# A causal mask moved from TensorE to VectorE, a subtraction from VectorE to GpSimd, and softmax exponents taken head by head with accumulated sums

## The reference

```
def _mha(x, kv, Wq, Wk, Wv, mask, causal):          # block 1: 16 heads of 8
    Q, K, V = (einsum('bsd,hdk->bhsk', t, W) * m ...)
    energy = einsum('bhsk,bhtk->bhst', Q, K)
    lengths = sum(energy[:, :, 0, :] != 0, axis=-1)
    energy = where(cols >= lengths, -inf, energy)
    if causal:
        energy = where(cols[None, :] > cols[:, None], -inf, energy)
    score = softmax(energy / sqrt(dk), axis=-1)
    return einsum('bhst,bhtk->bhsk', score, V) * m
x1 = layernorm(x + mha(x, x, Wq1, Wk1, Wv1, mask0, causal=True))
x2 = layernorm(x1 + mha(x1, context, Wq2, Wk2, Wv2, mask1, causal=False))
x3 = layernorm(x2 + ffn(x2))
# block 2: 16 heads of 64; bias and graph_attn_bias are the same input f
scores = einsum('bhqd,bhkd->bhqk', (x3 @ wq + bq) / 8, ctx @ wk + bk) + f + f
weights = softmax(scores, axis=-1)
out = layernorm(einsum('bhqk,bhkd->bhqd', weights, ctx @ wv + bv) @ wo + bo + x3)
```

## Time and profile before

| | |
|---|---|
| median of 3 runs | 341.50 us (341.49 to 341.51) |
| the profiled execution | 341.61 us, of which the trace spans 339.8 us |
| PE busy | 320.3 us, 94% of the span |
| DVE busy | 291.3 us, 86% |
| ACT busy | 239.9 us, 71% |
| POOL busy | 241.6 us, 71% |
| granted TensorE clock, mean | 0.995 |

### The profile page before, as it was taken

The page is one execution under the profiler, slowest core; times in us unless marked ns, Lnnn a source line. Parts: engine busy times, 40 slices in busy tenths (PEclk is TensorE's granted clock), DMA queues, the critical chain, the costliest instruction groups (busy, mean ns, idle before and its releaser), DMA issues.

```text
span 339.8 us, 13231 instructions
## 1 busy us (share of the span) xinstructions
PE 320.3 (94%) x5328; PEld 252.3 (74%) x5333; DVE 291.3 (86%) x836; ACT 239.9 (71%) x567; POOL 241.6 (71%) x376
## 2 busy tenths in 40 slices
PE   6799999999999989999999999999999999999982
PEld 2467668786869787878878787877878687867762
DVE  3776998999999999999999898989998989885661
ACT  1677768587787867778867876787785978776541
POOL 0453385676898858786978779687778679788773
PEclk9999999999999999999999999999999999999998
DMA  5996000010003000210100040001200040004001
GB/s 154 332 327 210 3 0 2 3 65 4 2 4 133 2 4 2 88 57 12 54 4 3 2 141 4 11 3 33 103 2 5 0 143 3 3 17 136 2 2 31
DMA packets 13180, 17.87 MB, mean 53 GB/s; under 512 B 1601, under 2 KB 10177, under 8 KB 13121
## 3 DMA queue, kind: packets, MB, share of 16 engines
q1 hardware_dynamic: 13120, 17.04, 15.8%
HBM read 15.99 MB, written 1.05 MB: 50 GB/s over the span
## 4 chain that ended last, share of the span: by engine, by line
PE 56%; DVE 26%; ACT 5%; issue 5%; POOL 4%; DMA 1%; SPq 1%; POOLq 0%; ACTq 0%; DVEq 0%
PE C_E L632 5%; PE C_E L577 4%; PE B_E L451 3%; PE C_E L622 3%; PE A_E L432 3%; PE B_E L432 3%; PE C_E L593 2%; DVE A_mx L889 2%; PE A_E L451 2%; DVE A_S L897 2%; PE C_E L609 2%; PE B_E L465 2%; DVE Sc L973 2%; DVE C_den L991 2%; DVE L_xh L943 2%
## 5 line engine op out<-in xcount | busy, mean ns | idle before, releaser
L1025 POOL TENSOR_TENSOR A_kblk<-A_qk,cst 128x1024 f32<-128x1024 f32 x16 | 30.3, 1897 | 25.5 <-DVE A_qk L865 25.4
L1046 POOL TENSOR_TENSOR L_xg<-L_xh,vec_sb 128x128 f32<-128x128 f32 x64 | 29.2, 456 | 15.9 <-DVE L_xh L943 13.9
L1035 POOL TENSOR_TENSOR L_rstd<-L_ve,cst 128x1 f32<-128x1 f32 x64 | 35.1, 548 | 5.0
L1077 POOL TENSOR_TENSOR Sc<-Sc,C_mx 128x512 f32<-128x512 f32 x28 | 29.1, 1046 | 9.4 <-DVE C_mx L983 9.3
L763 ACT ACTIVATE qT<-C_E,bq 128x128 f32<-128x128 f32 x112 | 31.9, 379 | 4.1 <-PE C_E L577 3.9
L1033 POOL TENSOR_TENSOR L_ve<-L_mv,cst 128x1 f32<-128x1 f32 x64 | 12.1, 189 | 29.4 <-DVE L_mv L930 28.8
L1086 POOL TENSOR_TENSOR Pc<-Pc,C_rd 128x512 f32<-128x512 f32 x28 | 29.0, 1043 | 2.8 <-DVE C_rd L993 2.5
L1025 POOL TENSOR_TENSOR B_kblk<-B_qk,cst 128x1024 f32<-128x1024 f32 x16 | 30.3, 1897 | 0.0
L577 PE MATMUL C_E<-x3T,wq_sb 128*128 128x128 f32 x224 | 29.6, 279 | 0.4 <-ACT x3T L755 0.4
L577 PEld LDWEIGHTS C_E<-x3T,wq_sb 128*128 128x128 f32 x224 | 27.0, 192 | 1.1 <-ACT x3T L755 0.7
L632 PE MATMUL C_E<-wo_sb,C_zT 128*128 128x128 f32 x224 | 27.5, 276 | 0.1
(11 more groups left out here) (186 smaller groups left out, 1002.4 us busy)
## 6 DMA issues: line engine op xcount, KB each, us to landing
f<-in_fs SPq DMA_DIRECT2D x16, 512.0 KB, 4.0
out<-osb SPq DMA_DIRECT2D x16, 64.0 KB, 1.8
cTs<-in_ctxT SPq DMA_DIRECT2D x1, 768.0 KB, 9.2
xTs<-in_xT SPq DMA_DIRECT2D x1, 768.0 KB, 6.8
xs<-in_x SPq DMA_DIRECT2D x1, 768.0 KB, 9.0
cs<-in_ctxn SPq DMA_DIRECT2D x1, 768.0 KB, 11.2
vec_sb<-in_vecs SPq DMA_DIRECT2D x1, 640.0 KB, 7.8
wk_sb<-in_wk SPq DMA_DIRECT2D x1, 512.0 KB, 4.5
```

The source lines that it names most:

```text
L1025: tt(a.kblk[:], a.qk[:, 1].unsqueeze(1).to_broadcast([P, 8, P]), at["rmask"].unsqueeze(2).to_broadcast([P, 8, P]), ALU.mult).then_inc(a.s_ ...
L1035: tt(l.rstd[:], l.ve[:], at["power"], ALU.pow).then_inc(l.s_rstd, 1)
L1046: tt(l.xg[:], l.xh[:], l.g, ALU.mult).then_inc(l.s_xg, 1)
L1077: tt(v, v, place(n).mx[:, 8 * g:8 * g + 8].unsqueeze(2).to_broadcast([P, 8, S]), ALU.subtract).then_inc(C.s_sub, 1)
```

## The change

Four edits, and a new `PLAN` for them:

- The mask is no longer added by PE. DVE adds `later` (now f32) to the scores as it moves them from PSUM to `A.S` (`A.msk_0`, `A.msk_1`), then takes the maxima from `A.S`, and the subtraction of the maxima, in place in `A.S`, goes to POOL (`a_sub`).
- In C's second half (`_1`), POOL no longer subtracts the maxima from 512 columns but multiplies the eight maxima by -2; ACT takes the exponents in eight ACTIVATEs of 64 columns with that as bias, and each also writes its head's sum (`accum_out`) to `den`; DVE then only takes the reciprocal. The first half (`_0`) stays as it was.
- `A.m0`'s comparison takes a tensor of zeros in place of the number 0.
- `COOL` goes from 6 to 9: nine `L.warm` steps of three products instead of six.

```diff
-COOL = 6
+COOL = 9
...
-            def energy(a, l, causal):
+            def energy(a, l):
...
-                                      a.kblk[r, :, S * b:S * b + S], start=True, stop=not causal,
-                                      skip_group_check=True)
-                    if causal:
-                        for hf, bank in enumerate((a.E, a.X)):
-                            r = slice(S * hf, S * hf + S)
-                            for b in range(2):
-                                last = mm(bank[S * b:S * b + S, :], eye64[r, :],
-                                          later[r, :].unsqueeze(1).to_broadcast([S, 8, S]),
-                                          start=False, stop=True, skip_group_check=True)
+                                      a.kblk[r, :, S * b:S * b + S], start=True, stop=True)
                     last.then_inc(a.s_e, 1)
...
             def c_exp(g):
                 def step(n):
+                    o = place(n)
+                    if g == 0:
+                        act.wait_ge(C.s_sub, 2 * n + 1)
+                        act.activation(o.P[:, 0:HALF], o.S[:, 0:HALF], ACT.Exp, scale=2.0).then_inc(C.s_p, 1)
+                    else:
+                        act.wait_ge(C.s_sub, 2 * n + 2)
+                        for h in range(8, 16):
+                            last = act.activation(o.P[:, h * S:(h + 1) * S], o.S[:, h * S:(h + 1) * S], ACT.Exp, scale=2.0,
+                                                  bias=o.mx[:, h:h + 1], accum_out=o.den[:, h:h + 1])
+                        last.then_inc(C.s_p, 1)
...
-                ts(m0s[:, n:n + FIRST], am0[:, n:n + FIRST], 0.0, None, ALU.is_gt).then_inc(s_m0, 1)
+                tt(m0s[:, n:n + FIRST], am0[:, n:n + FIRST], blank[:, 0:FIRST], ALU.is_gt).then_inc(s_m0, 1)
...
+            def masked(hf):
+                def step(n):
+                    dve.wait_ge(A.s_e, n + 1)
...
+                    tt(heads(A.S[:, hf * HALF:(hf + 1) * HALF]), heads((A.E, A.X)[hf][:, :]),
+                       later[:].unsqueeze(1).to_broadcast([P, 8, S]), ALU.add).then_inc(A.s_msk, 1)
+            def masked_max(hf):
+                def step(n):
+                    dve.wait_ge(A.s_msk, 2 * n + 1 + hf)
+                    dve.tensor_reduce(A.mx[:, 8 * hf:8 * hf + 8], heads(A.S[:, hf * HALF:(hf + 1) * HALF]), AX.X, ALU.max
+                                      ).then_inc(A.s_max, 1)
...
-                    dve.tensor_reduce(d, heads(place(n).P[:, g * HALF:(g + 1) * HALF]), AX.X, ALU.add).then_inc(C.s_den, 1)
-                    dve.wait_ge(C.s_den, 2 * n + 1 + g)
+                    if g == 0:
+                        dve.tensor_reduce(d, heads(place(n).P[:, 0:HALF]), AX.X, ALU.add).then_inc(C.s_den, 1)
+                        dve.wait_ge(C.s_den, n + 1)
                     dve.reciprocal(place(n).rd[:, 8 * g:8 * g + 8], d).then_inc(C.s_rd, 1)
...
                     pool.wait_ge(C.s_max, 2 * n + 1 + g)
+                    if g == 1:
+                        m = place(n).mx[:, 8:16]
+                        tt(m, m, at["twice"].to_broadcast([P, 8]), ALU.mult).then_inc(C.s_sub, 1)
+                        return
...
+            def a_sub(hf):
+                def step(n):
+                    pool.wait_ge(A.s_max, 2 * n + 1 + hf)
+                    v = heads(A.S[:, hf * HALF:(hf + 1) * HALF])
+                    tt(v, v, A.mx[:, 8 * hf:8 * hf + 8].unsqueeze(2).to_broadcast([P, 8, S]),
+                       ALU.subtract).then_inc(A.s_sub, 1)
```

More of the change, by code:

```diff
@@ L58 @@
 WARM = 6
-COOL = 6
-CONST = dict(ident=P, hmask=H, rmask=H // 2, bsel=2, trow=1, own=2, power=1, eps0=1, eps1=1)
+COOL = 9
+CONST = dict(ident=P, hmask=H, rmask=H // 2, bsel=2, trow=1, own=2, power=1, eps0=1, eps1=1, twice=1)
 def by_half(fs):
@@ L75, in constants @@
         "rmask": (p[:, None] % S) // DK0 == np.arange(H // 2)[None],
+        "twice": np.full((P, 1), -2.0),
         "bsel": p[:, None] // S == np.arange(2)[None],
@@ L105, in bass_two_blocks @@
         ofb = sb("ofb", [P, 2], BF16)
-        eye64, later = sb("eye64", [P, S], BF16), sb("later", [P, S], BF16)
+        later = sb("later", [P, S])
         iota = sb("iota", [P, S])
@@ L636, in _ @@
             steps = {"K.warm": warm_first, "L.warm": warm_last, "B.tr": b_tr, "B.f1": f1, "B.f2": f2, "B.f3": f3, "C.x3t": c_x3t, "C.e": c_e, "C.zt": c_zt, "C.o": c_o, "C.bvo": bvo,
[L637 to L638 removed]
+                     "A.qkv": qkv(A, [W[n] for n in ("Wq1", "Wk1")]), "A.e": energy(A, L1),
+                     "B.qkv": qkv(Bc, [W[n] for n in ("Wq2", "Wk2")]), "B.e": energy(Bc, L2)}
             for g in range(2):
@@ L804, in _ @@
             dve.tensor_copy(ofb[:], at["bsel"]).then_inc(ready, 1)
-            ts(later[:], iota[:], at["trow"], BIG, ALU.is_gt, ALU.mult)
-            ts(eye64[:], iota[:], at["trow"], None, ALU.is_equal).then_inc(ready, 1)
+            ts(later[:], iota[:], at["trow"], BIG, ALU.is_gt, ALU.mult).then_inc(ready, 1)
             def wlo(n):
@@ L1008, in _ @@
             for nm, a in (("A", A), ("B", Bc)):
-                steps |= {nm + ".q0": q0(a), nm + ".v": v(a), nm + ".nz": nz(a), nm + ".cut": cutk(a), nm + ".zn": zn(a),
-                          nm + ".max_0": maximum(a, 0), nm + ".max_1": maximum(a, 1),
-                          nm + ".sub_0": sub(a, 0), nm + ".sub_1": sub(a, 1)}
+                steps |= {nm + ".q0": q0(a), nm + ".v": v(a), nm + ".nz": nz(a), nm + ".cut": cutk(a), nm + ".zn": zn(a)}
             for g in range(2):
+                steps |= {f"A.msk_{g}": masked(g), f"A.max_{g}": masked_max(g),
+                          f"B.max_{g}": maximum(Bc, g), f"B.sub_{g}": sub(Bc, g)}
                 steps |= {f"C.fadd_{g}": fadd(g), f"C.max_{g}": c_max(g), f"C.den_{g}": den(g)}
@@ L1260 @@
-C.rstd#15 C.xh#15 C.gb#15 C.store#15
+A.qkv#0 A.qk#0 A.q0#0 A.e0#0 A.nz#0 A.cnt#0 K.warm#0 A.cut#0 C.whi#0 A.v#0 K.warm#1 A.kblk#0 C.chi#0 C.wlo#0
+A.qkv#1 C.wvhi#0 C.clo#0 A.e#0 K.warm#2 A.qk#1 A.msk_0#0 C.k_0#0 A.q0#1 A.max_0#0 C.k_1#0 C.ks_0#0 A.msk_1#0
+A.sub_0#0 A.e0#1 C.ks_1#0 A.max_1#0 C.k_0#1 A.exp_0#0 A.nz#1 A.sub_1#0 A.m0#0 C.k_1#1 C.wvlo#0 A.pt_0#0
+A.exp_1#0 A.cnt#1 A.pts_0#0 A.pt_1#0 A.v#1 A.pv_0#0 A.pts_1#0 A.cut#1 C.ks_0#1 A.pv_1#0 A.kblk#1 A.qkv#2
+A.zts#0 C.ks_1#1 A.z#0 C.k_0#2 A.zn#0 C.k_1#2 A.y#0 C.ks_0#2 A.st#0 K.warm#3 C.ks_1#2 C.k_0#3 A.rstd#0 C.chi#4
@@ new lines @@
+C.k_1#3 A.xh#0 C.ks_0#3 A.gb#0 A.e#1 C.ks_1#3 C.clo#4 B.am#0 C.v_0#0 A.msk_0#1 B.cm#0 A.qk#2 C.v_1#0 C.vs_0#0
+A.max_0#1 B.tr#0 A.msk_1#1 C.k_0#4 A.sub_0#1 B.xts#0 C.vs_1#0 A.q0#2 A.max_1#1 A.e0#2 A.exp_0#1 A.sub_1#1
+C.k_1#4 A.nz#2 C.ks_0#4 A.cnt#2 B.qkv#0 A.exp_1#1 A.v#2 A.pt_0#1 B.qk#0 A.pt_1#1 B.q0#0 A.pts_0#1 B.e0#0
+A.pts_1#1 A.pv_0#1 C.ks_1#4 B.nz#0 A.pv_1#1 A.cut#2 K.warm#4 A.zts#1 A.kblk#2 A.z#1 C.k_0#5 A.zn#1 B.cnt#0
+K.warm#5 A.y#1 C.ks_0#5 A.st#1 A.qkv#3 C.k_1#5 B.v#0 A.rstd#1 C.k_0#6 C.ks_1#5 A.xh#1 B.cut#0 A.gb#1 A.e#2
@@ new lines @@
+C.nrm_1#13 B.f1#15 B.f1s#15 B.f2#15 C.gb#11 C.pt_1#13 B.f2s#15 B.f3#15 C.pts_1#13 C.x3c#13 C.store#11
+C.qs_1#14 B.y3#15 C.rstd#12 C.zt#13 C.loadf#13 B.3st#15 C.xh#12 C.e#14 B.3rstd#15 C.zts_0#13 C.zts_1#13
+B.3xh#15 C.o#13 C.fadd_0#14 B.3gb#15 C.max_0#14 C.fadd_1#14 C.sub_0#14 C.x3t#15 L.warm#0 C.max_1#14 C.x3ts#15
+C.exp_0#14 C.y#13 L.warm#5 C.sub_1#14 C.exp_1#14 C.den_0#14 C.q_0#15 C.q_1#15 C.nrm_0#14 C.qs_0#15 C.den_1#14
+C.st#13 L.warm#4 C.nrm_1#14 C.pt_0#14 C.qs_1#15 C.pt_1#14 C.pts_0#14 C.e#15 C.pts_1#14 C.zt#14 C.fadd_0#15
@@ L1261 @@
+C.max_0#15 L.warm#3 C.zts_0#14 C.fadd_1#15 C.zts_1#14 C.sub_0#15 L.warm#2 C.max_1#15 L.warm#1 C.exp_0#15
+C.sub_1#15 C.o#14 C.x3c#14 C.exp_1#15 C.den_0#15 C.rstd#13 C.nrm_0#15 C.den_1#15 C.nrm_1#15 C.pt_0#15 L.warm#6
+C.pts_0#15 C.gb#12 C.pt_1#15 L.warm#7 C.xh#13 C.pts_1#15 C.y#14 C.store#12 C.st#14 C.zt#15 L.warm#8 C.rstd#14
+C.x3c#15 C.zts_0#15 C.gb#13 C.zts_1#15 C.xh#14 C.o#15 C.gb#14 C.store#14 C.store#13 C.y#15 C.st#15 C.rstd#15
+C.xh#15 C.gb#15 C.store#15
 """.split()
```

308 lines of the change are left out of this document (149 added, 159 removed).

## The result

The changed kernel takes 353.0 us against 341.5 us before, 1.033 times as long (95% interval 1.0295 to 1.0364). The forecast was 338.9 us, with a range up to 344.5; it was wrong in sign.

What follows compares the result with a forecast made beforehand. PE and DVE, both nearly full, were taken to lead in turn in the middle; mask -2.8, sums -2.7 and end +2.9 gave -2.6 us from 341.61, so 339.0, as median 338.9 us, range 334.0 to 344.5.

Steps and rivals of the forecast that it cites:

- ACT's exponents: Chain C's second half: eight heads take 2.7 us, 2.1 us more a pair (1.2 to 3.8), hidden in the middle.
- the sum: Whole kernel: -2.8 (mask), -2.7 (sums), +2.9 (end) make -2.6 us.
- The end: Last pairs, 14 and 15, chain C: the eight heads are not hidden there; 2.9 us later (1.1 to 6.2).
- The mask: Chain A's scores on PE: mask gone saves 0.31 us at nine pairs, 2.8 us (2.0 to 3.6).
- DVE's sums: Second-half sums of 667 ns leave DVE in the middle; four count, saving 2.7 us (0 to 8.0).
- POOL's part: Chain A's subtractions on POOL, less C's second half: net 1.24 us more a pair, covered, taken as nothing.
- DVE's part of the mask: Chain A on DVE: an addition replaces the subtraction, the maximum gets no dearer; nothing saved or lost.
- The zero-row test: Four-number comparison on DVE: by the skill's contention rule nothing saved, taken as nothing; bound 1.9 us.
- The forecast's own range: Whole kernel: 335 to 340.8 us, from masks 2.0 to 3.6, sums 0 to 4, end 1.1 to 4.
- ACT becomes the bound: slower: Rival: PE's copies wait behind ACT's eight-head blocks, decisive from about 0.5 us a head; 346.8 us, chance 0.29.

Runs made afterwards that it cites:

- b_freeheads: Kernel before, old order: second half's subtraction and sum gone, one 512-column exponent with one bias, per-head maxima left out; 341.0 us, ratio 0.9971.
- f_maskpe: a_freeheads with the mask back on PE and chain A's subtraction back on DVE; 343.5 us, ratio 1.0032.
- a_freeheads: Changed kernel with the eight exponents as one of 512 columns with one bias, second half's per-head maxima and sums left out; 341.7 us, ratio 0.9996.
- a_neither: Changed kernel with mask on PE, chain A's subtraction on DVE and one 512-column exponent as before; new order, zero-row test, idle steps kept; 355.1 us.
- b_mask: Kernel before in its own order, with only the mask moved to DVE and chain A's subtraction to POOL; 362.1 us, ratio 1.0584.
- f_sum: a_freeheads with DVE summing the second half of each pair as in the kernel before; 347.8 us, ratio 1.0163.

## Why the prediction was wrong

The way from the kernel before to the changed one can be walked in four steps, each between two runs, by their ratios: the second half's subtraction and sum taken out in the old order (b_freeheads), -1.0 us; the new order (f_maskpe; with it the new form of the zero-row test and the nine idle steps), +2.1; the mask moved (a_freeheads), -1.2; the block of eight exponents with sums in place of one (the changed kernel), +11.4. The sum is 11.3 us, the loss by its ratio. Another way through the runs divides it differently: the new order alone, with the old instructions, loses 12.8 us (a_neither), and the changed instructions then give back 1.5. So it is not the block alone: in the new order the old instructions of the second half find no room either.

- **ACT's exponents, the step that failed.** The price was right: 2.7 us forecast, 2.77 measured, taken from the copies' rows. What failed is the sentence behind it: "In the middle ACT's idle time is 52.8 us, 4.4 a pair; it goes to 195 of 223 us. At my price this is hidden." It isn't. Idle time counts only where it lies; behind the block stand copies that PE waits for, and only part of the 2.1 us found cover. The block costs 11.4 us, where the sum has 2.9, all of it at the end. The same step priced the new order at the end only.
- **The end.** The timeline of the changed kernel, last two pairs:

```profile
327.26 0.63 ACT L767 ACTIVATE Pc<-Sc 128x512 f32<-128x512 f32 x1 [0.23 <-POOL Sc L1102]
...
330.44 2.12 ACT L757 ACTIVATE A_kblk<-A_E,bq 128x128 f32<-128x128 f32 x8
...
332.61 1.16 PE L587 MATMUL A_E<-kT,A_kblk 64*64 64x64 f32 x64
...
336.41 0.63 ACT L767 ACTIVATE A_S<-A_S 128x512 f32<-128x512 f32 x1 [0.53 <-POOL A_S L1102]
...
340.01 1.04 POOL L1120 TENSOR_TENSOR A_S<-A_S,C_rd 128x512 f32<-128x512 f32 x1 [0.89 <-DVE C_rd L1014]
```

From pair 14's first exponent to pair 15's scores it is 5.35 us, and was 317.18 to 320.94, 3.76: 1.6 later, forecast 1.9. From pair 15's first exponent to the end of its normalization it is 4.64 us, and was 3.72 (325.08 to 328.80): 0.9 more, as worked out. Between them the way from scores to exponent is 0.3 shorter. In all 2.2 us for the forecast 2.9. This term was right.
- **The mask.** With all that it brings to DVE and POOL it gives 1.2 us, give or take 0.8 by the two intervals (1.8 by the medians), where the sum has 2.0 to 3.6. The four products without it hold PE for 1.02 us on the chain, as forecast:

```profile
24.85 1.02 PE A_E L434 x8
```

- **DVE's sums.** Forecast 2.7 us (0 to 8.0). In the new order with ACT out of the way they are worth 5.7, in the old one at most 1.0 together with POOL's subtraction. So the size hangs on the order, and the forecast mixed the two: it read from the old order's chain what would be gained in the new one.
- **POOL's part and DVE's part of the mask.** POOL's nothing holds in the new order (352.6 against 353.0), and not in the old one, where the subtraction costs 15 us. The reason given, that a round of the other chains lies between, holds in both orders, so it was not enough. That the new order alone makes the cover is not shown: in b_mask POOL also keeps the second half's subtraction, 0.85 us a pair more than in the changed kernel, and ACT has no block. On DVE the prices were right (685 ns for the addition and 681 for the maximum, against 683 and 667); what its new steps cost was not tried by itself.
- **The new order as such.** The prediction priced it only at the end. With the second half cheap and the mask on PE it costs 2.1 us against the old order. Why it has no room on the way of chain C's second half, where the old order had (1.0 us there, 11.6 here from f_maskpe to a_neither), stays open: two lists of 1,900 words differ, and the mixed lists tried only start and end.
- **The zero-row test.** The tile `m0s` in the changed kernel (min/median/max ns):

```profile
L838 DVE TENSOR_TENSOR m0s<-am,blank x4: 163/434/1377, 17.9 to 173.0; 128x4 f32<-128x4 f32 x4
```

It still takes up to 1.4 us for four numbers, as it took up to 1.0 before, so nothing was saved there. The timelines show what holds it. Of the kernel before, and of the changed one:

```profile
17.42 1.90 POOL L1025 TENSOR_TENSOR A_kblk<-A_qk,cst 128x1024 f32<-128x1024 f32 x1 [3.89 <-DVE A_qk L865]
18.54 0.81 DVE L838 TENSOR_SCALAR m0s<-am 128x4 f32<-128x4 f32 x1
...
172.50 1.04 POOL L1120 TENSOR_TENSOR Pc<-Pc,C_rd 128x512 f32<-128x512 f32 x1
173.00 0.55 DVE L838 TENSOR_TENSOR m0s<-am,blank 128x4 f32<-128x4 f32 x1
```

The test ends 0.03 and 0.01 us after a POOL instruction that was running when it began; the other four long tests of the two kernels do the same. For the new form, with two inputs in SBUF, this agrees with the rule of the Trainium skill weighed in the prediction (SBUF — State Buffer, section Who interferes with whom). The old form, with one, was held in the same way, so the rule as quoted does not tell the two forms apart.
- **The range.** The forecast's own range, 335 to 340.8 us, does not follow from its terms: masks at 2.0, sums at 0 and the end at 4 give 343.5.

**The rival.** "ACT becomes the bound: slower" had the mechanism, "the copies that PE waits for stand behind blocks", and a chance of 0.29. Its condition was wrong: it was to decide from 0.5 us a head, and decided at 0.33, since it was worked out from ACT's total time and from the end, not from what the block holds up.

No version that computes the whole result beats the kernel before. In the new order the fastest of them is f_sum, 347.8 us: one exponent of 512 columns whose bias is one head's maximum for all eight (a constant per row that the softmax divides out, as long as nothing overflows), with the sums on DVE.
